# Local attention: softmax weights divided on GpSimd, the heads' output copied by VectorE, output projection moved ahead of the transposes

## What is computed

```
for l in range(2):                        # _layer
    h = shift_token(x)                    # second half of the columns from the token before
    q, k, v = split(h @ wqkv)             # 8 heads of 64
    q, k = rotary(l2norm(q) * qs), rotary(l2norm(k) * ksc)
    attn = softmax(mask(q k^T * 8))       # windows of 64 tokens: own window and the one before
    x = x + (attn v) @ wo                 # 512 -> 128
    x = x + ffn(layernorm(shift_token(x)))
```

## Time and profile before

| | |
|---|---|
| median of 3 runs | 2665.46 us (2664.93 to 2665.88) |
| the profiled execution | 2669.65 us, its span 2667.9 us |
| PE busy | 2175.1 us (82%) |
| DVE busy | 1967.1 us (74%) |
| ACT busy | 1435.0 us (54%) |
| POOL busy | 584.0 us (22%) |
| granted TensorE clock, mean | 0.913 |

### The profile page before, as it was taken

One profiled execution on the slowest core, in us unless ns is written; L12 is line 12 of the kernel. 1 busy time (PEld: TensorE's weight loads), 2 busy tenths in 40 slices (PEclk: granted clock), 3 DMA queues, 4 the chain that ended last, 5 costly groups with the idle time before them and its releaser, 6 DMA issues.

```text
span 2667.9 us, 46774 instructions
## 1 busy us (share of the span) xinstructions
PE 2175.1 (82%) x17520; PEld 1235.2 (46%) x17520; DVE 1967.1 (74%) x4192; ACT 1435.0 (54%) x2637; POOL 584.0 (22%) x400
## 2 busy tenths in 40 slices
PE   3799689878779959988779977997877995898777
PEld 3667312354647712246465741225564672223645
DVE  4865789678675589967777469967877657996677
ACT  1234267674733427766653335777473342776755
POOL 0062100124134200040405320004312531003050
PEclk9999779989879969999888987998987996999889
DMA  4000200011000020010100021001100003001010
GB/s 151 0 1 1 72 26 10 15 23 30 15 10 1 2 83 18 10 30 5 31 21 1 1 60 31 18 6 31 24 15 18 1 1 84 18 10 29 7 30 21
DMA packets 58920, 63.92 MB, mean 24 GB/s; under 512 B 17136, under 2 KB 44080, under 8 KB 58160
## 3 DMA queue, kind: packets, MB, share of 16 engines
q1 hardware_dynamic: 55480, 57.77, 8.6%
q10 hardware_dynamic: 3192, 2.90, 0.3%
HBM read 25.19 MB, written 15.01 MB: 15 GB/s over the span
## 4 chain that ended last, share of the span: by engine, by line
PE 47%; DVE 28%; ACT 14%; issue 6%; DMA 2%; SPq 2%; POOL 0%; DVEq 0%; ACTq 0%; POOLq 0%
PE PS L1350 44%; DVE arena L1105 10%; ACT arena L715 7%; DVE arena L1204 2%; ACT arena L658 1%; PE PS L1675 1%; DVE tmp L1179 1%; DVE s_at L1179 1%; DVE arena L1172 1%; PE PS L1368 1%; DMA tmp<-xf 1%; ACT tmp L669 1%; DVE arena L1291 1%; SPq L329 1%; ACT arena L723 1%
## 5 line engine op out<-in xcount | busy, mean ns | idle before, releaser
L1350 PE MATMUL PS<-arena 128*32 128x256 f32 (+4 forms) x10240 | 807.7, 349 | 132.7 <-DVE arena L1105 50.1
L1105 DVE TENSOR_REDUCE arena<-PS 128x1 f32<-128x512 f32 x1024 | 640.5, 685 | 41.1 <-PE PS L1350 41.1
L658 ACT ACTIVATE arena<-PS 128x1024 f32<-128x1024 f32 x512 | 517.9, 1028 | 174.1 <-PE PS L1350 173.0
L1350 PEld LDWEIGHTS PS<-arena 128*32 128x32 f32 (+4 forms) x10240 | 309.2, 121 | 626.0 <-DVE arena L1105 265.6
L610 ACT ACTIVATE arena<-PS 128x512 f32<-128x512 f32 x256 | 150.8, 597 | 244.2 <-PE PS L1350 244.0
L1350 PEld LDWEIGHTS PS<-w2e,arena 128*128 128x128 f32 x2048 | 246.0, 192 | 50.6 <-issue 49.8
L1350 PE MATMUL PS<-w2e,arena 128*128 128x128 f32 x2048 | 247.7, 275 | 0.3
L715 ACT ACTIVATE arena<-PS,arena 128x128 f32<-128x128 f32 x512 | 230.9, 546 | 22.3 <-DVE arena L1241 20.9
L1068 DVE TENSOR_TENSOR arena<-PS,arena 128x512 f32<-128x512 f32 x128 | 86.2, 689 | 208.5 <-PE PS L1350 208.1
L1350 PE MATMUL PS<-wqkv,arena 128*128 128x512 f32 x384 | 179.4, 607 | 25.5 <-ACT arena L697 21.7
L465 POOL TENSOR_TENSOR zz<-zz,arena 128x512 f32<-128x512 f32 x104 | 135.4, 1302 | 265.4 <-DVE arena L1068 236.6
(11 more groups left out here) (301 smaller groups left out, 3435.3 us busy)
## 6 DMA issues: line engine op xcount, KB each, us to landing
arena<-arena SPq DMA_DIRECT2D x120, 128.0 KB, 2.3
scr_q<-arena SPq DMA_DIRECT2D x40, 128.0 KB, 2.5
scr_k<-arena SPq DMA_DIRECT2D x40, 128.0 KB, 2.4
arena<-scr_k SPq DMA_DIRECT2D x24, 200.0 KB
arena<-scr_q SPq DMA_DIRECT2D x24, 192.0 KB
x_in<-in_x SPq DMA_DIRECT2D x5, 512.0 KB, 4.0
out_x<-tmp SPq DMA_DIRECT2D x4, 512.0 KB, 3.9
wqkv<-in_wqkv SPq DMA_DIRECT2D x1, 1536.0 KB, 7.1
```

The lines of the kernel that those rows point to most:

```text
L658: act.activation(pb[:, n % 8], pair(2 * (n % 2)), ACT.Exp).then_inc(S["p"], 1)
L1105: dve.tensor_reduce(mxp[:, h % 2, j, t, hf:hf + 1], PS[:, ring_bank("mx", h, n), :], AX, ALU.max)\
L1350: return pe.matmul(o, w, v, start=start, stop=stop, **kw)
```

## The change

The division of the weights is split: DVE takes the reciprocal of the sums (new semaphore `rlr`), POOL multiplies. The copy of the heads' output into `olT` leaves ACT and becomes the first statement of DVE's turn u, for tile u-4. On PE the output projection of tile u-4 stands right behind the heads' products of tile u-3, ahead of the transposes of tile u-2. The waits that each piece of work had go with it.

```diff
@@ pool
+                    for u in range(T):
+                        m = l * T + u
+                        pool.wait_ge(S["rlr"], m + 1)
+                        v = pl[:, m % 3]
+                        pool.tensor_tensor(v, v, bc(rl[:, m % 3], [P, 2, 4, KEYS], 3), ALU.mult).then_inc(S["pn"], 1)
@@ act
-                    for u in range(T + 4):
+                    for u in range(T + 2):
...
-                        if 3 <= u <= T + 2:
-                            q = n - 3
-                            act.wait_ge(S["o_lps"], q + 1)
-                            if q >= 2:
-                                act.wait_ge(S["ol_ps"], q - 1)
-                            act.copy(olT[:, q % 2], PS[:, 6, :].rearrange("p (c n) -> p c n", c=4))\
-                                .then_inc(S["olT"], 1)
@@ dve
                     for u in range(T + 6):
                         n = T * l + u
+                        if 4 <= u <= T + 3:
+                            q = n - 4
+                            dve.wait_ge(S["o_lps"], q + 1)
+                            if q >= 2:
+                                dve.wait_ge(S["ol_ps"], q - 1)
+                            dve.tensor_copy(olT[:, q % 2], PS[:, 6, :].rearrange("p (c n) -> p c n", c=4))\
+                                .then_inc(S["olT"], 1)
                         if 2 <= u <= T + 1:
                             m = n - 2
                             dve.wait_ge(S["p_exp"], 8 * (m + 1))
-                            link(dve.reciprocal(rl[:, m % 3], sl[:, m % 3]))
-                            v = pl[:, m % 3]
-                            dve.tensor_tensor(v, v, bc(rl[:, m % 3], [P, 2, 4, KEYS], 3), ALU.mult).then_inc(S["pn"], 1)
+                            if m >= 3:
+                                dve.wait_ge(S["pn"], m - 2)
+                            dve.reciprocal(rl[:, m % 3], sl[:, m % 3]).then_inc(S["rlr"], 1)
@@ tensor
                             ins.then_inc(S["o_lps"], 1)
+                        if 4 <= u <= T + 3:
+                            t = u - 4
+                            q = l * T + t
+                            pe.wait_ge(S["olT"], q + 1)
+                            pe.wait_ge(S["xf"], 2 * T * l + t)
+                            for c in range(4):
+                                ins = mm(PS[:, 7, 0:W], olT[:, q % 2, c], res["wol"][:, l, c],
+                                         start=(c == 0), stop=(c == 3))
+                            ins.then_inc(S["ol_ps"], 1)
                         if 2 <= u <= T + 1:
                             m = n - 2
                             pe.wait_ge(S["pn"], m + 1)
...
```

More of the change, by code:

```diff
@@ L240, in build @@
         st_ps p pv on on_moved ot_ps tn ob_ps otn xab op_ps op_rd x2 s1
-        sh_ps hsh0 hsh1 hcp_v hT_ps hT hT_late qkv_ps sq rotb rqe qkr kq_ps kq vl s_lps ml p_exp pn ssq ssq_ok rq0 rot vz ptd pt_ps pt o_lps olT ol_ps xf
+        sh_ps hsh0 hsh1 hcp_v hT_ps hT hT_late qkv_ps sq rotb rqe qkr kq_ps kq vl s_lps ml p_exp rlr pn ssq ssq_ok rq0 rot vz ptd pt_ps pt o_lps olT ol_ps xf
         ffn_tile g_ps a_ps gl hg y2_ps xb gfin obuf
@@ L1757, in _ @@
                                 ins.then_inc(S["pt_ps"], 1)
[L1758 to L1766, removed]
                     def last_shift(t, o):
```

## The result

The changed kernel takes 2821.27 us (median of 4 runs, 2815.51 to 2838.47) against 2665.67 us for the kernel before on the same chip: a ratio of 1.0595, 95% interval 1.0548 to 1.0642. It is 156 us slower; 139 were forecast.

A forecast was written before the change was run, and what follows sets the result against it. ACT looked like the bound of a steady 4.44 us turn, PE 0.2 us behind. Chain, hold and clock summed to 8 x (11.4 + 3.2 + 2.8) = 139 us, giving 2805 us, range 2745 to 2840 (8 times in 10).

The forecast's parts named there:

- the projection moves ahead of the transposes: On PE, the projection idles 2.56 us for DVE's copy, reciprocal, maxima, `ml` and addition, with the transposes queued behind it.
- the bare chain: PE and DVE waiting on each other through the moved projection and copy: +11.4 us a layer, 91 us in all.
- The rounds: Times from one DVE residual addition to the next: 6.92 us first, then 5.41 twice, 5.30 twice, about 1.65 at the end.
- links: Single pieces of the PE and DVE wait, timed from profile rows, such as projection 1.06 us and hop to DVE 0.11.
- The hold of `ml`: On DVE, `ml` is delayed by POOL's product: 0.8 us in turns 4 to 7, 3.2 a layer, 26 in all.
- The product: POOL's 128x1024 multiplication with a broadcast operand: 1.95 us each, itself hidden because the transposes come later.
- The clock: PE's clock drops after long idle gaps: one and a half spells, +2.8 us a layer, 22 in all; bounds 0 and 3.8.
- a sign that I had given for being wrong: On PE, the forecast would be wrong if the clock stayed down past turn 8.
- clock down all through: Rival: PE at half clock for six rounds, +19 us a layer on top of 11.4 and 3.2; 2934 us, 4 in 100.
- Chain without side costs: Rival: PE and DVE waits alone, `ml` not held and clock up; 2756 us, 10 in 100 near this low end.
- The stall ends with the scores: Rival: PE stalls only in turns 5 and 6, the tail as before; some 8 us a layer, 2730 us, 7 in 100.
- ACT's relief: Rival: removing ACT's copy makes it faster, 0.2 us in each of four turns, 2659 us, or 2650; 2 in 100.

The follow-up runs named there:

- order_back: The changed kernel with PE's projection put back behind the transposes; 2732.38 us, ratio 1.0249 to the kernel before.
- add_first: The changed kernel with the residual addition and the small work behind it first in DVE's turn, ahead of the copy; 2695.94 us, ratio 1.0108.
- late_filler: The filler kernel with DVE's reciprocal moved behind `ml`; 2753.47 us, ratio 1.0330 to the kernel before.
- filler: The changed kernel with useless matmuls put in PE's idle time between the heads' products and the projection; 2780.37 us, ratio 1.0419.
- recip_late: The changed kernel with DVE's reciprocal moved behind `ml`; 2823.50 us, ratio 1.0576 to the kernel before.
- between: Kernel before with POOL dividing, PE order scores, transposes, heads, projection, heads' copy for tiles 0 to 3 at DVE's turn end, others on ACT; 2639.36 us, ratio 0.9891.
- copy_only: The kernel before with only the copy of the heads' output moved from ACT to the head of DVE's turn; 2787.56 us, ratio 1.0445.

## Why the prediction was right, and where its sizes were off

*The path.* The forecast was 2805 us, and 2821 were measured. The step "the projection moves ahead of the transposes" held as written. The wait is 3.18 us in turns 5 and 6; 2.56 and the hold of 0.8 made 3.4. Order_back and add_first show it from both sides: either the transposes go back ahead of the wait or the addition goes ahead of the copy, and 89 or 125 us come back. The three edits together cost 156 us. Alone they cost 0 (POOL), 38 (order) and 119 (copy): the copy at the head was the heaviest, and the addition and DVE's second copy both stand behind it. That 0, 38 and 119 add up to nearly 156 is chance, for POOL and copy together cost 66 and not 119.

*The terms.* Late_filler has neither hold nor clock loss. It stands 86 us above its before; 91 were forecast for the bare chain (+11.4 us a layer; by layers, 456.7 less 376.2 is 10.1 each). The first addition comes 1.3 us later than before, where 1.85 were forecast. The rounds were 6.78 (6.92 forecast), then 5.19, 5.22 (5.41), 5.11, 5.20 (5.30). Two links were taken too long: with the transposes behind it the projection takes 0.97 us of PE (587.40 to 588.37 in the changed kernel), where 1.06 were taken from a row with scores behind it, and the copy starts 0.03 us after the heads end (584.23 to 584.26), where 0.11 were taken.

The hold of `ml` was put at 26 us, 0.8 in each of four turns. It is 27 (filler less late_filler), or 23 by the layers alone, and the row of `ml` is longer by 0.70 us in four turns. The product takes 1.90 us, 1.95 were taken. In the changed kernel the hold cannot be read from the total, as recip_late showed. By the rule of the Trainium skill (SBUF — State Buffer, "Who interferes with whom") a VectorE instruction with two SBUF inputs and a GpSimd instruction that reads SBUF exclude each other until the first of them is through; the traces agree, `ml` ending 0.03 us after POOL. The estimate of 2.13 us for the product, from the Trainium skill (GPSIMD Engine Reference, section 2.1), was further off than the 1.95 from the rows.

The clock was put at 22 us with a bound of 3.8 us a layer; it is 41 (changed kernel less filler, 2821 to 2780), or 5.1 us a layer, beyond that bound. This is the term that was mis-sized; the chain, forecast 5 us too long, makes up for a quarter of it, and so far the nearness of the total is luck. I counted one and a half spells a layer in the two rounds with long gaps, and let the clock be up in the tail. In the profiled execution it was down in the tail too: the second and third rounds are 6.8 to 7.8 us in all eight layers, where filler has 5.2, and in the first and fifth layer the fourth and fifth rounds are 6.8 us as well. So a sign that I had given for being wrong, the clock down past turn 8, came in these two layers: in the first, the projections of turns 9 and 10 (616.33 and 623.17) still take 1.93 and 1.94 us. The third and seventh layer have it back for the fourth and fifth rounds and lose it again in the last two, 2.24 and 2.52 us where the second and fourth layer have 1.66 and 1.60. The first and fifth layer cost 22 and 25 us more than before, still less than the 33.6 of the rival "clock down all through". The spread of the changed kernel's runs, 23 us, is of this origin as far as can be seen: the mean granted clocks of its four runs, 0.885, 0.893, 0.894 and 0.897, go with 2838, 2824, 2819 and 2816 us, and filler spreads over 7.6 us.

*What is left over.* The eight layers explain 151 of the profiled execution's 169 us. The other 18 lie between the passes and layers, less 4 us that are won ahead of the first: from a second layer's last addition to the next pass's first maxima it takes 478 to 479 us before and 481, 483 and 484 us after. The stretch between the two layers of a pass is 68 us, where it was 65 to 66. In filler, where the stretch between passes is 481 to 483 us, the clock comes back some 20 us later in it: at the same distance from the layer's end two windows of 20 us have 0.65 and 0.83, and before 0.84 and 1.00. late_filler has 478 us there. Why the same work meets another clock from kernel to kernel stays open.

*The rivals.* "Chain without side costs" fell: both side costs are there. Its 2756 us are the price of the chain by itself, and late_filler has 2753. "The stall ends with the scores" fell: the tail's rounds are 5.1 to 5.3 us even at full clock. Its own sum was wrong as well: 1.85, 2.5 and the side costs of 3.2 and 2.8 make 10.3 us a layer and 2748 us, not 8 and 2730. ACT's relief did not decide anything in the changed kernel: in the first layer ACT waits 3.03 and 3.68 us before it comes to the exponentials of tiles 6 and 7. What it is worth once the ring is broken, as in between, was not measured by itself.

## What to carry to other kernels

On engines with an order written by hand, what counts of a moved statement is what stands behind it, and what it waits for by way of another engine's order; busy shares show neither. Draw the ring (who waits for whom, once round, with start-to-start times of the rows) for each edit and for the edits together, before moving anything: here it gave, within 6 us, the time of a version that is faster, and within 13 us those of all runs but recip_late and copy_only, which came out 25 and 28 us above their forecasts; in both the clock was down, and the links had left it out. Put work that waits for the longest ring last on its engine, and ask of every new idle time on PE what it does to the clock.

## What the runs showed that was not expected

A gap on PE does not always lower the clock. In recip_late's first layer a wait of 2.49 us ahead of the projection was followed by a window at 0.57, and a second wait of 2.48 us eight microseconds later by full clock; in order_back two waits of 2.15 and 2.16 us cost nothing. In filler, where only 0.53 us of the 3.2 us between heads and projection are idle, it stayed at full. What decides it is not shown.

POOL's product also seems to hold a copy from SBUF to SBUF, with one input. In between, the small copy behind the addition of tile 2 took 1.70 us, against 0.18 for the one of the turn before. It starts after the product of that turn and ends 0.04 us after it (timelines of DVE and POOL):

```profile
592.54 0.18 DVE L1222 COPY tmp<-xf 128x64 f32<-128x64 f32 x1
...
594.36 1.70 DVE L1222 COPY tmp<-xf 128x64 f32<-128x64 f32 x1
```

```profile
594.12 1.90 POOL L504 TENSOR_TENSOR arena<-arena 128x1024 f32<-128x1024 f32 x1 [2.61 <-DVE arena L1239]
```

It happens twice in every layer of between and in no other of the runs with POOL's product; what it costs there was not measured.
